# A four-part graph network on one core: function set loaded ahead, mask work a turn later, shorter bursts in the sort, half of the one-hots remade on VectorE

## Time and profile before

| | |
|---|---|
| median of 3 runs | 9191.92 us (9173.51 to 9197.65) |
| profiled execution | 9174.3 us, span 9172.8 us |
| PE busy | 6676.0 us (73%) |
| PE weight loads busy | 5135.1 us (56%) |
| DVE busy | 5985.6 us (65%) |
| ACT busy | 3335.7 us (36%) |
| POOL busy | 3246.3 us (35%) |
| mean granted TensorE clock | 0.808 of full |
| DMA | 1330.15 MB, mean 145 GB/s |

### The profile page before, as it was taken

How to read it: one execution, slowest core, us unless ns; L and a number is a source line. 1 busy time by engine, 2 the same in 40 slices (tenths; PEclk the granted TensorE clock), 3 DMA queues, 4 the chain that set the end, 5 groups by cost and what they waited for, 6 DMA issues and landing times. The chain is left out here.

```text
span 9172.8 us, 305358 instructions
## 1 busy us (share of the span) xinstructions
PE 6676.0 (73%) x86569; PEld 5135.1 (56%) x86577; DVE 5985.6 (65%) x18295; ACT 3335.7 (36%) x5533; POOL 3246.3 (35%) x5198
## 2 busy tenths in 40 slices
PE   5899999344435766666667667666688899899887
PEld 4566665233324655555556456555566577677666
DVE  7445544799996766666666667566677555455677
ACT  2444444122223333433433433333344233233343
POOL 3666666444422443443444344344200000000254
PEclk9888988655556777777777677777799899899999
DMA  3666666233344775675677576577544111111487
GB/s 97 168 172 176 180 174 173 65 82 82 83 152 121 192 190 163 188 190 164 173 198 203 141 197 184 159 190 191 147 147 144 61 64 65 45 65 64 118 229 203
DMA packets 1790244, 1330.15 MB, mean 145 GB/s; under 512 B 1259701, under 2 KB 1482604, under 8 KB 1780410
## 3 DMA queue, kind: packets, MB, share of 16 engines
q1 hardware_dynamic: 1149466, 924.40, 33.4%
q0 software_dynamic: 261536, 328.49, 14.1%
q10 hardware_dynamic: 379008, 74.48, 4.6%
HBM read 1034.27 MB, written 291.36 MB: 145 GB/s over the span
## 5 line engine op out<-in xcount | busy, mean ns | idle before, releaser
L521 POOL DMA_DIRECT2D big<-rows x3384 | 1842.4, 545 | 4218.5 <-issue 2393.9
L1277 PE MATMUL ps<-big 128*128 128x64 bf16 x31584 | 2017.0, 209 | 1152.9 <-DVE big L1737 716.6
L1277 PEld LDWEIGHTS ps<-big 128*128 128x128 bf16 x31584 | 1586.9, 104 | 1556.5 <-issue 1287.3
L1266 PE MATMUL ps<-big 128*128 128x64 bf16 x31584 | 1346.0, 206 | 119.5 <-DVE big L1701 51.4
L1266 PEld LDWEIGHTS ps<-big 128*128 128x128 fp8e4 x31584 | 1213.2, 106 | 239.9 <-issue 165.9
L1013 ACT CAST big<-big 128x512 bf16<-128x512 f32 x1128 | 697.0, 618 | 1728.6 <-DVE big L1714 1408.0
L783 POOL DMA_INDIRECT rows<-big x800 | 980.5, 1226 | 688.2 <-issue 344.7
L1714 DVE TENSOR_TENSOR big<-ps,big 128x512 f32<-128x512 f32 x940 | 648.9, 690 | 582.4 <-DMA big<-rows 316.8
L1019 ACT CAST big<-big 128x512 bf16<-128x512 f32 x1316 | 813.0, 618 | 582.7 <-issue 431.1
L1737 DVE TENSOR_TENSOR big<-big 128x512 bf16<-128x512 f32 x1316 | 902.7, 686 | 4.2 <-ACT big L1019 3.5
L1502 DVE SCALAR_TENSOR_TENSOR big<-big 128x1000 f32<-128x1000 f32 (+1 forms) x300 | 359.3, 1198 | 700.3 <-ACT big L905 700.1
(11 more groups left out here) (256 smaller groups left out, 8880.5 us busy)
## 6 DMA issues: line engine op xcount, KB each, us to landing
big<-ohdD SPq DMA_DIRECT2D x658, 512.0 KB, 4.3
big<-ohsD SPq DMA_DIRECT2D x658, 256.0 KB, 2.8
big<-rows POOLq DMA_DIRECT2D x3384, 32.0 KB, 3.4
big<-rows SPq DMA_DIRECT2D x3384, 32.0 KB, 3.4
big<-maskD SPq DMA_DIRECT2D x50, 1600.0 KB, 6.6
big<-rows ACTq DMA_DIRECT2D x2256, 32.0 KB, 3.3
big<-keyT SPq DMA_DIRECT2D x100, 488.3 KB
ohdD<-big SPq DMA_DIRECT2D x188, 256.0 KB, 2.5
```

The source lines that it names most:

```text
L521: eng.dma_start(edge[:, s.r, j, :], rows[bass.ds(v[s.r * (hi - lo) + j - lo], P), col]).then_inc(landed[s.r], 16)
L1266: last = pe.matmul(pG[g.r][:, j * D:(j + 1) * D], ohsR[:, g.r, j * P:(j + 1) * P].bitcast(F8), slices[:, g.r, q // QUAD, c * D:(c + 1) * D ...
L1277: last = pe.matmul(pacc[:, bass.ds(w[j], D)], hot[:, g.r, j * P:(j + 1) * P], parts[:, g.r, c, j * D:(j + 1) * D], start=False, stop=False ...
```

## The change

Four edits.

1. ACT loads the function set of the logarithm once, ahead of each layer's edge pass (`preload_act_table`).
2. DVE's part of the mask work (`fix_counts`) runs one turn later than ACT's: `steps` has a new argument `late`, by which DVE unrolls one more turn ahead of the loops.
3. The burst of zero matmuls is 12 only in steps with j = 0; in the other three of four it is 2.
4. Only the first four tiles (QUAD) of each group's dst one-hots go to `ohdD` and come back into `hot`. POOL keeps the masked dst numbers in a new array `dstl` (bf16, one more operation a group in the unpack stage); DVE makes the other four tiles of `hot` from them, by one comparison of 128x512 values a group (`remake`), at the end of its step, for group s-2. PE's `scatter` waits for it too (`hot_made`).

```diff
-        ohdD = dram("ohdD", (NG, P, GT * P), BF16)
+        ohdD = dram("ohdD", (NG, P, QUAD * P), BF16)
...
+        dstl = big[:, BIG - TILES // 2:].bitcast(BF16)
...
-        def steps(eng, body, aside=None):
-            for i in range(2 * U):
+        def steps(eng, body, aside=None, late=0):
+            for i in range((2 + late) * U):
                 body(Step(i // U, i % U))
-            cuts = [2] + ([2 + (k + 1) * UNITS for k in range(MASKS)] if aside else []) + [TRIPS]
+            cuts = [2 + late] + ([2 + late + (k + 1) * UNITS for k in range(MASKS)] if aside else []) + [TRIPS]
...
-                sp.wait_ge(hots_ready, i * 2 + 2)
+                sp.wait_ge(hots_ready, i * 2 + 1)
...
-                             ohD[:, r, :, :].rearrange("p a b -> p (a b)")).then_inc(dst_stored[r], 16)
+                             ohD[:, r, 0:QUAD, :].rearrange("p a b -> p (a b)")).then_inc(dst_stored[r], 16)
...
-                sp.dma_start(hot[:, s.r:s.r + 2, :], ohdD[bass.ds(s.i, 2)].rearrange("g p f -> p g f")).then_inc(hot_loaded[s.r // 2], 16)
+                sp.dma_start(hot[:, s.r:s.r + 2, 0:QUAD * P], ohdD[bass.ds(s.i, 2)].rearrange("g p f -> p g f")).then_inc(hot_loaded[s.r // 2], 16)
...
+                pool.tensor_tensor(dstl[:, span], rowst[:, r, :, 1], valid[:, span], ALU.mult)
                 for k in range(2):
...
                 act.wait_ge(w_free, l + 1)
                 hold(act)
+                act.preload_act_table(ACT.Ln)
                 edge_pass(l * NG, False, bass.ds(l * D + D, D), log_counts)
...
-                    for _ in range(12 if m == 0 else 0):
+                    for _ in range(0 if m else 12 if j == 0 else 2):
                         pe.matmul(bank(4), zerob[:, :], each(iota1b[:, :], 4), start=True, stop=True)
...
                     pe.wait_ge(lo_ready, base + g.i + 1)
+                    pe.wait_ge(hot_made, base + g.i + 1)
...
+            def remake(s, base):
+                if s.live(2):
+                    g = s.lag(2)
+                    if not g.known or g.i >= RING:
+                        dve.wait_ge(scattered, base + g.lag(RING).i + 1)
+                        hold(dve)
+                    dve.tensor_tensor(hot[:, g.r, QUAD * P:].rearrange("p (a b) -> p a b", a=QUAD), each(iota1b[:, :], QUAD),
+                                      over(dstl[:, bass.ds(g.i * GT + QUAD, QUAD)], P), ALU.is_equal).then_inc(hot_made, 1)
...
                     lower(s, l * NG)
+                    remake(s, l * NG)
...
-                steps(dve, body, fix_counts)
+                steps(dve, body, fix_counts, 1)
...
                     lower(s, base)
+                    remake(s, base)
```

More of the change, by code:

```diff
@@ L250, in graph_kernel @@
         total = carve(W)
+        assert carve.at[0] <= BIG - TILES // 2
         carve = carver()
@@ L388, in graph_kernel @@
         lo_ready = sem("lo_ready")
+        hot_made = sem("hot_made")
         hot_loaded = [sem(f"hot_loaded{r}") for r in range(RING // 2)]
```

## The result

The changed kernel takes 9331.81 us (median of five, 9280.71 to 9353.74), the kernel before 9173.51 (five, 9172.61 to 9197.65) on the same chip. The ratio is 1.016 with a 95% interval of 1.013 to 1.019: slower by 1.6%, where the prediction had it faster. The time lies inside the predicted range and away from the forecast. The profiled execution took 9280.71 (span 9278.6), 106 us more than the profiled one of before. By the medians the loss is 158 us; the other four executions of the changed kernel took 43 to 73 us more than the profiled one, at a mean granted clock of 0.752 to 0.756 against 0.761, and where those further microseconds lie no profile shows.

What follows compares the result with a forecast made beforehand. No engine was taken as full overall: PE stalls and slow clock in the sort, DVE in unpack, waits in L0. Terms -80 +3 +34 +20 -10 sum to -33 us, 9159 from the median, written as 9150; range 8990 to 9370.

Steps and rivals of the forecast that it cites:

- The sort, the step that failed: Sort: ten zero matmuls fewer in 75 of 100 steps save 0.8 us a step, -80 us, stalls taking the rest.
- Rival B: Sort: clock isn't regained after stalls without the burst; slow steps about 20 us, sort +170, total 9410; chance 0.11.
- Rival A: Sort gains nothing: the transfer loop sets 15.4 us a step; total 9230; chance 0.18.
- Mask turns: L0: ordinary mask turns 0.5 us longer, +80 us; first eight of a layer 15.97 to 15.0, -39 us.
- The sum for L0: L0: load ahead +6, ordinary mask turns +80, first eight -39, turns without mask 0, half load -13; +34 us.
- The function set: L0: forty table loads at L1013 and forty at L1052 go, five come; first message possibly late, +6 us.
- The remake: DVE: one bf16 comparison of 512 elements in each of 1316 groups, at the single rate, 0.60 us each.
- rival D: DVE: the remake runs at twice the rate, 0.30 us instead of 0.60; total 8895; chance 0.11.
- Rival C: DVE: the remake isn't hidden; half hidden costs 0.30 us a group, +285 us, total 9445; chance 0.10.
- PE's new wait for hot_made: PE's scatter: the awaited group is made two DVE steps before its lower part finishes, so the wait costs nothing.
- L1 and L3: L1: 2.78 us a group, +20 us. L3: 2.81 us a group with less DMA traffic, -10 us.
- Unpack: Unpack stage: one more POOL operation of 0.20 us a group, half the bytes stored, DVE stays the bound; +3 us.

Runs made afterwards that it cites:

- e_none: Changed kernel with no zero matmuls at all in the sort; ratio 1.032 to the kernel before, 18.20 us a sort step.
- e_long: Changed kernel with the old burst of twelve zero matmuls back in every sort step, other three edits kept; ratio 1.0015 to the kernel before.
- e_fullload: Changed kernel with the long burst, whole one-hots stored and loaded, DVE's comparison still made into an unread spare buffer; ratio 1.011 to the kernel before.
- e_setlate: Kernel before with only the function set loaded ahead and DVE's mask operations one turn later; ratio 0.990 to the kernel before.
- e_late: Kernel before with only DVE's mask operations one turn later; ratio 0.990 to the kernel before.
- e_halfload: Changed kernel with the long burst and half load, DVE remaking only the first four groups of a pass; ratio 0.981 to the kernel before.

## Why the prediction was wrong

**The sort, the step that failed.** The term was -80 us; the profiled run has +99 (16.42 less 15.42, times 99). The prediction took the burst as 2.3 us of PE work to be saved a step, and let transfers and stalls eat half of it. The saving was priced right: full-clock steps took 11.3 us. But the path it put beside it did not bind: stalls took 18 us in all instead of more than the 70 before. What failed is that the sum left the clock as it was: the burst is what brings the full clock back and keeps it, and without it whole steps ran at 19.8 us. Rival B had the clock not coming back behind a short burst, at 0.11. It had the slow step right (about 20 us; 19.8 measured) and its point of decision (from about 20 slow steps on; there were 19, and many more partly slow), but tied the slow clock to stalls and priced the sort at +170. The rows say otherwise: stalls fell from 26 to 11 and the clock fell all the same, 31 of 41 times with no stall ahead. B's argument against itself, that L1 holds the full clock without a burst, was the misleading one: L1's matmuls stream 64 bf16 columns on 128 rows, the sort's are mostly fp32 with mixed shapes, and e_none shows that these alone do not bring the clock back. Whether it is fp32 or the shape was not separated. Rival A, steps still at 15.4, fell too.

**Mask turns.** In the layer shown, ordinary ones went from 14.50 to 15.10, predicted 15.0, and the first eight from 15.97 to 15.09, predicted 15.0. Over the five passes the 32 ordinary turns got longer by 0.52 us on average (14.84 to 15.36), as foretold. Turns behind the mask work took 12.26 us before and 11.72 after, where the prediction had nothing (it counted 30 turns without mask work; 7 of each layer's 47 make 35); e_long has 11.69 and e_fullload 12.36, so the half load gave it. The sum for L0 was +34, measured +32.6. The split behind it was less good. The two edits give -18 us a pass and the remake with its half load +25 (e_setlate, e_long). On an ordinary turn the stall's removal alone gave 0.11 us, not its 0.56, and the remake with its half load on top took 0.63. The prediction had added up DVE's whole order with the remake in it, and that sum holds; what the stall is worth without the remake it did not ask.

**The function set.** The forty loads at L1013 and forty at L1052 went and five came (1283 ns each, idle before them 0.1). The first eight turns gained as counted, but the gain does not need this edit: the later mask operations alone hide the loads too (e_late).

**The remake.** 684 ns, spaced 0.60: taken at 0.60, rival D refuted. Before the run no row showed such an operation; now one does, and the rule of the Trainium skill ("VectorE: DVE Perf Modes", What auto-detection actually checks) that two 16-bit results a cycle want steps of 1 or -1 in every tensor agrees with it. Both operands of this one are bf16 and it still takes as long as the f32 operations beside it (0.68). Rival C, half of the remake not hidden (0.30 us a group, +285), did not come: against e_setlate, e_fullload gives 31.6 us a pass in L0, 0.17 us a group, nearer to the 0.12 counted, and 0.06 and 0.04 in L1 and L3.

That PE's new wait for hot_made cost nothing is read from the code and the waits; no run leaves the wait alone out. PE's idle before its scatters, before and after:

```profile
PE ps L1277 <- DVE big L1737: 716.6, 327, 5.0
PE ps L1277 <- issue: 344.3, 403, 2.7
```
```profile
PE ps L1284 <- DVE big L1753: 674.4, 227, 4.0
PE ps L1284 <- DVE big L1702: 385.8, 392, 3.5
PE ps L1284 <- issue: 58.3, 51, 3.3
```

The second line of after looks like a new wait of 386 us. By the code it is none: the remake of a group is issued two steps ahead of its lower part, so what was put down to issue before (344.3) very likely has another name now (385.8 with 58.3 left). The sums are 1061 and 1118; the 58 us between them are not placed.

**L1 and L3.** Predicted +20 and -10, measured +2 and -21 (500.5 to 502.3, 535.8 to 514.5). In L1 DVE runs at 464 of 470 us, 2.683 us a group, just under the 2.70 added up from rows: a full engine, and PE's chain added nothing to it, where +0.08 a group was allowed. In L3 fewer bytes gave more than assumed (e_halfload -22.7).

**Unpack.** +3 predicted, -9.5 measured. e_halfload, with the extra POOL operation, shows the same (904.1), e_fullload, with it and the whole store, 913.9: the half store, or SP's shorter wait with it, gave it, and the POOL operation cost nothing. POOL's wait for DVE there went from 378.7 us to 336.1.

```profile
POOL big L804 <- DVE big L1619: 336.1, 178, 4.4
```

With the sort's term as measured (+99 for -80) the prediction's own sum is 9174.3 + 99 + 3 + 34 + 20 - 10 = 9320; measured were 9281, so the other terms were off by 39 us in all, towards a better time. That the time lies inside the range at all is the rivals' doing: the forecast's own part of it ended at 9215.

## What to carry to other kernels

Work on TensorE that looks like filler may be holding the clock for everything behind it: before cutting it, find in the trace what precedes each return to the full clock, and price the cut with a whole step at half the clock, not only with the filler's own time. A busy engine in the profile does not mean a full clock; read the granted clock beside it. Of several edits on one wait, try each alone: here one of two gave all of the gain, and an edit that moves work from transfers to VectorE paid only in the stage where transfers were the limit.

## What the runs showed that was not expected

- PE at 98% busy (e_none, 1459 of 1484 us) stayed at the slow level of 1.2 GHz in nearly all of the sort, mean granted clock 0.52.
- Of 19 bursts of twelve bf16 zero matmuls (512 columns, 128 rows) that began at the slow clock, 18 ended at the full one (the one shown took 4.20 us); twelve on 32 rows took 5.3 us a step, and the fastest of the 200 transposes behind them took 415 ns.
- Stalls did not set the mean clock: with 11 of them instead of 26 it was 0.69 instead of 0.90, and 31 of 41 falls had none ahead.
- A DVE comparison with a repeated operand takes 684 ns for 512 elements with all-bf16 data, as with f32.
- Eighty table loads of 1283 ns cost nothing that could be measured once DVE used the result a turn later (e_late 0.9897 with them, e_setlate 0.9905 without).
